# Attention beside a three-layer network: the network's matmuls in half-row pairs over two PSUM banks, and a new rule for when value products are taken

## The reference

```python
def _L0_attn_ref(x, w_qkv, b_qkv, w_out, b_out):
    qkv = x @ w_qkv + b_qkv
    q, k, v = jnp.split(qkv, 3, axis=-1)          # then 16 heads of 16 features
    scores = jnp.einsum('bhid,bhjd->bhij', q, k) * attn_scale
    scores = jnp.where(j >= i, scores, -jnp.inf)
    attn = jax.nn.softmax(scores, axis=-1)
    out = jnp.einsum('bhij,bhjd->bhid', attn, v)
    return out @ w_out + b_out

def _L0_ffn_ref(x, k0, k1, k2, s0, s1, s2):      # k0 512x1024, k1 1024x1024, k2 1024x256, all +-1
    h = jnp.concatenate([x, -x], axis=-1)
    h = s0 * _conn_dense(k0, h)
    h = jax.nn.relu(h) * 2
    h = s1 * _conn_dense(k1, h)
    h = jax.nn.relu(h) * 2
    return s2 * _conn_dense(k2, h)

xn = _layernorm(x, axis=-1)
x = x + _L0_attn_ref(xn, ...) * _silu(_L0_ffn_ref(xn, ...))
```

## Time and profile before

| what | us |
|---|---|
| time, median of 3 runs (lowest, highest) | 2429.61 (2428.54, 2431.49) |
| the profiled execution's own time | 2430.44 |
| its span, first to last instruction | 2428.7 |
| PE busy | 2363.3 |
| weight loads (PEld) busy | 1482.5 |
| DVE busy | 1792.3 |
| ACT busy | 1525.4 |
| POOL busy | 913.9 |

### The profile page before, as it was taken

How to read it: one execution, slowest core, us unless ns; L and a number is a source line. 1 busy time by engine, 2 the same in 40 slices (tenths; PEclk the granted TensorE clock), 3 DMA queues, 4 the chain that set the end, 5 groups by cost and what they waited for, 6 DMA issues and landing times.

```text
span 2428.7 us, 50993 instructions
## 1 busy us (share of the span) xinstructions
PE 2363.3 (97%) x17616; PEld 1482.5 (61%) x17616; DVE 1792.3 (74%) x4516; ACT 1525.4 (63%) x3135; POOL 913.9 (38%) x1080
## 2 busy tenths in 40 slices
PE   7999999999999999999999999999999999999995
PEld 6777666656565656565655656566665666555652
DVE  7767777777777777777877777777777777777732
ACT  5664656667666676666666666666666666666552
POOL 1005334343333434343434434353434444344533
PEclk9999999999999999999999999999999999999997
DMA  8983112020111212131212112221212212122222
GB/s 307 353 326 112 37 33 58 24 64 23 45 39 43 77 53 78 39 87 39 82 46 74 55 39 76 56 79 41 77 44 68 63 37 83 49 73 78 62 72 81
DMA packets 157805, 192.67 MB, mean 79 GB/s; under 512 B 65276, under 2 KB 102076, under 8 KB 157560
## 3 DMA queue, kind: packets, MB, share of 16 engines
q1 hardware_dynamic: 156600, 189.41, 25.4%
q10 hardware_dynamic: 960, 0.00, 0.0%
HBM read 112.13 MB, written 76.14 MB: 78 GB/s over the span
## 4 chain that ended last, share of the span: by engine, by line
PE 90%; DMA 4%; DVE 2%; issue 1%; SPq 1%; ACT 1%; POOL 1%; POOLq 0%; ACTq 0%; DVEq 0%
PE b_ps L1342 22%; PE b_pv_ps L1320 22%; PE b_ps L1300 15%; PE b_ps L1288 15%; PE b_ps L1346 5%; PE b_ps L1339 5%; DMA a_xs<-L_attn_x 3%; PE b_ps L1365 3%; PE a_qk_ps L290 1%; DVE a_stats L396 1%; DVE a_qk_parts L434 1%; PE b_ps L1308 1%; PE a_v_ps L300 0%; ACT b_probs L1400 0%; SPq L1133 0%
## 5 line engine op out<-in xcount | busy, mean ns | idle before, releaser
L1400 ACT ACTIVATE b_probs<-b_ps 128x512 f32<-128x512 f32 (+3 forms) x2560 | 1184.1, 541 | 622.2 <-PE b_ps L1288 613.3
L1455 DVE TENSOR_REDUCE b_part_max<-b_ps 128x1 f32<-128x512 f32 x1536 | 960.8, 680 | 279.2 <-PE b_ps L1300 276.0
L1452 DVE CUSTOM_DVE_ANT_0 b_ps<-b_ps,k_mask 128x512 f32<-128x512 f32 (+3 forms) x1024 | 477.2, 518 | 214.3 <-PE b_ps L1300 212.7
L1320 PE MATMUL b_pv_ps<-b_probs,k_vst 128*32 128x512 f32 (+3 forms) x5120 | 583.7, 540 | 0.6 <-ACT b_probs L1400 0.5
L1342 PE MATMUL b_ps<-b_u_hi,k_w 128*128 128x256 f32 x2048 | 535.6, 298 | 0.0
L1288 PE MATMUL b_ps<-k_qst,k_kst 50*128 50x512 f32 (+3 forms) x2560 | 503.5, 411 | 7.2 <-ACT b_u L1428 3.7
L1300 PE MATMUL b_ps<-k_kst,k_qst 48*128 48x512 f32 (+3 forms) x2560 | 494.5, 410 | 3.3 <-DVE b_part_max L1455 0.9
L1342 PE MATMUL b_ps<-b_u_lo,k_w 128*128 128x256 f32 x2048 | 497.3, 279 | 0.0
L1342 PEld LDWEIGHTS b_ps<-b_u_hi,k_w 128*128 128x128 f32 x2048 | 386.7, 189 | 81.1 <-issue 72.2
L1300 PEld LDWEIGHTS b_ps<-k_kst,k_qst 48*128 48x128 f32 x2560 | 234.6, 185 | 299.4 <-issue 152.1
L1288 PEld LDWEIGHTS b_ps<-k_qst,k_kst 50*128 50x128 f32 x2560 | 244.9, 185 | 255.4 <-ACT b_probs L1400 84.7
(11 more groups left out here) (105 smaller groups left out, 1847.8 us busy)
## 6 DMA issues: line engine op xcount, KB each, us to landing
qk_parts<-a_qk_parts SPq DMA_DIRECT2D x64, 512.0 KB, 3.9
k_kst<-qk_parts SPq DMA_DIRECT2D x384, 64.0 KB, 2.3
k_qst<-qk_parts SPq DMA_DIRECT2D x384, 64.0 KB, 2.3
a_xs<-L_attn_x SPq DMA_DIRECT2D x16, 512.0 KB, 6.0
xn_T<-a_xT SPq DMA_DIRECT2D x16, 512.0 KB, 5.8
v_plain<-a_v_out SPq DMA_DIRECT2D x16, 512.0 KB, 5.6
k_xf<-xn_T SPq DMA_DIRECT2D x32, 256.0 KB, 3.2
b_v_in<-v_plain SPq DMA_DIRECT2D x64, 128.0 KB, 2.7
```

The costliest lines, as they stand in the source:

```text
L1320: mm = pe.matmul(pv_ps[h * VW:(h + 1) * VW, 0:cols], vst[:, kb // TT, kb % TT, h, :], probs[:, s % P_SLOTS, h, 0:cols], start=start, stop= ...
L1400: act.activation(probs[:, s % P_SLOTS, h, 0:cols], ps[:, banks[place, half][0], 0:cols], ACT.Exp, scale=HD ** -0.5).then_inc(exp_done, 1)
L1452: dve.tensor_tensor_reduce(src, src, mask[:, 0:CHUNK - k0 % CHUNK], 1.0, -3.0e38, ALU.add, ALU.max, dst).then_inc(ring_read, 1)
L1455: dve.tensor_reduce(dst, src, AX_X, ALU.max).then_inc(ring_read, 1)
```

## The change

The network's blocks are cut in two halves of rows. A block's rows 0 to 63 and its rows 64 to 127 are two matmuls of 64 rows, as S and M have them, and since two row halves must not add into one bank at the same time, a use now has two banks: in the first half of the use, rows 0 to 63 add into the first bank and rows 64 to 127 into the second, for different output blocks; at half way they swap. So that the swap is safe, PE waits at half way for the last matmul of the first half (`f_half`). A use now covers four output blocks, 64 pairs in layer 1, 16 in layer 0 and 32 in layer 2, and there are five uses a piece, 160 in all. The matmuls of the network go from 6144 of 128 rows to 6144 pairs of 64 rows; the readers' work is the same but that the last layer's two ACT passes become four of half the width.

The plan's rules are new too. S, M and F are one mode now, and only V and the whole-array odds and ends change it. Values are taken once four steps wait, and then until none is left that is ready (`WAITING`, `LEFT`). Else the network goes first while it is behind its share, then an S or M pair if two banks are free, then the network, then values. A use of the network needs two free banks to begin.

```diff
-USES = KF // FPU
+F_BANKS = 2
+USES = KF // (F_BANKS * FPU)
...
+def network_pair(kind, j):
+    depth = KH if kind == "L0" else KF
+    phase, at = divmod(j, (1 if kind == "L2" else FPU) * depth * SPLIT)
+    return phase, at // (depth * SPLIT), at // SPLIT % depth, at % SPLIT
...
-        start = min(self.release)
+        start = sorted(self.release)[F_BANKS - 1]
...
-        if self.mode == "R":
-            self.begun = self.matmuls
-            if rows and pair <= now + self.STAY:
-                return "R"
...
+        if products and (waiting >= self.WAITING or self.mode == "V" and waiting > self.LEFT):
+            return "V"
+        if network and behind > 0:
+            return "F"
+        if rows and pair <= now:
+            return "R"
+        if network:
+            return "F"
+        if products and not (rows and pair <= now + 0.3):
             return "V"
...
-                    dst = f_bank(use)
+                    half_way = uses_of_network[use][3] // 2
                     for j in range(lo, hi):
...
+                        swapped, tile, f, part = network_pair(kind, j)
+                        if j == half_way:
+
+                            pe.wait_ge(f_half, use + 1)
+                        for n in range(F_BANKS):
+                            half = n ^ swapped
+                            rows = slice(half * HALF, (half + 1) * HALF)
...
+                                mm = pe.matmul(dst[:, tile], w[rows, f, m * P:(m + 1) * P], x_parts[part][rows, f, :],
+                                               start=first, stop=last, skip_group_check=True)
```

More of the change, by code:

```diff
@@ L627, in __init__ @@
         self.use = self.done = self.split = 0
-        self.matmuls = self.begun = 0
+        self.pairs = 0
         self.needed, self.split_at = {}, []
@@ L807, in take_network @@
                     self.emit(*event[2:])
-            self.take(("F", self.use), "f")
-        bank = self.banks["F", self.use][0]
-        count = min(count, total - self.done)
+            for n in range(F_BANKS):
+                self.take(("F", self.use, n), "f")
+        taken = [self.banks["F", self.use, n][0] for n in range(F_BANKS)]
+        count = min(self.QUANTUM, total - self.done)
         lo, self.done = self.done, self.done + count
@@ L821, in take_network @@
         if kind == "L2":
-            self.release[bank] = self.reads("ACT", self.clock["PE"], self.EXP, 1400)
-            self.clock["POOL"] = max(self.clock["POOL"], self.release[bank]) + 1.0
+            for bank in taken:
+                self.release[bank] = self.reads("ACT", self.clock["PE"], self.EXP, 900)
+            self.clock["POOL"] = max(self.clock["POOL"], self.release[taken[-1]]) + 1.0
             t = self.step()
@@ L829, in take_network @@
         else:
[L830 to L835, removed]
+            for bank in taken:
+                if self.split >= U_SLOTS:
+                    self.clock["ACT"] = max(self.clock["ACT"], self.split_at[self.split - U_SLOTS])
+                self.release[bank] = self.reads("ACT", self.clock["PE"], self.EXP, 640)
+                self.clock["POOL"] = max(self.clock["POOL"], self.release[bank]) + 1.95
+                self.split_at.append(self.clock["POOL"] + 0.1)
+                self.split += 1
             self.needed["L1" if kind == "L0" else "L2", k] = self.split
@@ L849, in choose @@
         waiting = self.scores // 2 - self.products
-        if self.mode == "R":
-            self.begun = self.matmuls
-            if rows and pair <= now + self.STAY:
-                return "R"
[L854 to L862, removed]
-            if products and waiting >= self.WAITING:
-                return "V"
-            if network:
-                return "F"
-        elif rows and free >= self.ENOUGH["V"]:
+        if products and (waiting >= self.WAITING or self.mode == "V" and waiting > self.LEFT):
[3 more added lines that the diff above has]
+        if rows and pair <= now:
             return "R"
-        if products:
+        if network:
+            return "F"
+        if products and not (rows and pair <= now + 0.3):
             return "V"
-        if network:
-            self.begun = self.matmuls
-            return "F"
-        return "R" if rows and pair <= now + 0.4 else None
+        return None
     def wait(self):
@@ L1325, in _ @@
                     if lo == 0:
-                        claimed(("F", use))
+                        for n in range(F_BANKS):
+                            claimed(("F", use, n))
                         if kind == "L0" and q == 0:
```

123 lines of the change are left out of this document (66 added, 57 removed).

## The result

The changed kernel takes **2475.85 us** (median of 4 runs, 2469.8 to 2480.05), the kernel before, run beside it, 2430.18 (4 runs, 2428.54 to 2431.49). The ratio is **1.0186**, 95% interval 1.0163 to 1.021: slower by 46 us, where 27 us less were forecast. It lies inside the range of the prediction, on the other side of no change.

A forecast was written before the change was run, and what follows sets the result against it. PE was taken as the bound, hardly ever idle in the second stage. The terms -224 + 6 + 20 + 180 + 31 - 40 = -27 took 2430.4 to 2403 us; forecast 2370 to 2435, whole range 2300 to 2525.

The forecast's parts named there:

- Changes of mode: PE's switches into R, the whole array and V become fewer, 374 us of cost down to 150: 224 saved.
- Half-row pairs: 6144 network matmuls become 6144 pairs of 256 columns, each 0.001 us dearer: +6 us, bounds 0 and 37.
- instruction issue: Rival: network pairs take four instructions for two, so 0.124 us a pair, 2434 us, about no change; chance 0.04.
- serial loads: Rival: the two halves' weight loads run one after the other, 657 us in place of 6, near 3050; chance 0.03.
- The wait at half way: PE waits 160 times, mid-use, for the first half's last matmul: +20 us, between 0 and 66.
- Pairs just in time: 1261 S and M pairs right behind a network pair, some with late weights: +31 us, between 0 and 126.
- late banks: The loader's 333 waits before S and M for a late bank in the kernel before go away: -40 us.
- The gaps: Between network uses PE runs short of banks while ACT and DVE read: +180 us, low bound 30, high bound 281.
- No time is to be had from the clock: PE's granted clock stood at 9 tenths or more in every slice but the last, so no gain there.
- The slower rival (2502): Gaps between uses and late pairs cost 238 us or more, against the forecast's 211: 2502 us; chance 0.37.
- The 0.09 behind a network pair: Sign: an S pair behind a network pair no longer pays the 0.09 us for leaving the network's mode.
- The loader's idle time before S and M: Sign: this idle time, released by ACT and DVE, rises from about 220 us by 150 or more, between uses.

The follow-up runs named there:

- the fastest kernel: The changed kernel with WAITING 5, LEFT 4 in place of 4, 0 (a single value step, only when five wait): 2370.35 us, ratio 0.976 to the kernel before.

## Why the prediction failed, point by point

**Changes of mode: -224 forecast, -223 to -226 found.** The prices from the earlier trace rows and the counts from the order were enough.

**Half-row pairs: +6 forecast, none found.** Pairs follow at 0.12 us (312.54 to 312.66), and 11 ns over the 107 of streaming fit the runs of pairs after as they fit the blocks before. Neither instruction issue nor serial loads showed.

**The wait at half way: +20 forecast, 14 to 17 found,** about 0.1 us a use; five or six uses touch low clock and are left out.

**Pairs just in time +31, late banks -40.** Together with the half-way wait and the pairs I had +17 within the uses; the excess there stayed the same (53.5 and 53.4; by the second sorting it fell by 9). The first term can be read from the trace: the 1031 S and M pairs that stand between network pairs of one use with no change of mode, the half-way places left out, hold 18 us of excess, where I had 31 for 1261. With the half-way wait that makes some 32 to 35, so 30 to 45 must have gone elsewhere within the uses, as the -40 has it. That is known by difference alone.

**The gaps: +180 forecast, +197 found,** about 207 with the waits that fall into low clock (204 and 217 by the second sorting). The account of the earlier trace rows against PE's own work was right to 10 or 20%, and the earlier trace rows, which spoke for 30, was rightly not followed: that stretch had begun with banks saved up.

**The clock: not in the sum, +66 found.** This is the step that failed: the sum has no term for the granted clock. "No time is to be had from the clock" is true of the earlier trace rows, and I read it as if none could be lost either. With the other terms as they came out the total would be -226 + 0 + 207 = -19, so 2411 against the 2403 of the forecast; with the clock it is +48. The trace of before had a warning. Windows before and after the clock falls in the middle of PE's one long wait for a reader:

```profile
core 0: us, PE busy (x) PEld busy (x) DVE busy (x) ACT busy (x) POOL busy (x), PEclk, DMA share, GB/s
2130.00:2141.20 11.20, 9.52 (x81) 6.30 (x79) 7.64 (x19) 6.20 (x12) 6.93 (x9) 1.00 0.07 15
2141.20:2148.00 6.80, 4.93 (x20) 3.78 (x20) 0.52 (x1) 3.23 (x7) 1.89 (x2) 0.50 0.31 87
```

And the timeline there:

```profile
2143.07 0.80 PE L1288 MATMUL b_ps<-k_qst,k_kst 50*128 50x512 f32 x2 [3.55 <-ACT b_u L1428]
2143.80 0.58 PE L1346 MATMUL b_ps<-k_w,b_u_hi 128*128 128x256 f32 x1
2144.18 0.41 PE L1346 MATMUL b_ps<-k_w,b_u_lo 128*128 128x256 f32 x1
2144.39 0.41 PE L1346 MATMUL b_ps<-k_w,b_u_hi 128*128 128x256 f32 x1
```

PE waited 3.55 us, up to 2143.07; the clock fell at 2141.2, within the wait, and PE then streamed at half speed, 0.21 us a matmul. I forecast 180 us of new waits and gave this no price. A third of the 66 us in the sum would have turned the forecast to no change (-27 + 22), and all of it to slower.

**The slower rival (2502).** The time went its way, but not by its mechanism: gaps and late pairs together came to some 215 to 235, under the 238 from which it was to decide, though not by much. What decided was the clock on top of them.

**The signs that I named.** Network pairs at 0.12: yes. The 0.09 behind a network pair is gone where the bank is free in time (312.06 to 312.23 still has 0.05 of it, as a late load). DVE's share of the second stage: 1663 of 2298 us, 72%, against 74% in the earlier trace rows; it fell, as it must where the time rises. The loader's idle time before S and M was a bad witness. Its causes before L1292 and then L1304, to be held against the earlier trace rows:

```profile
  ACT b_probs L1414: 81.0, 169
  DVE b_part_max L1472: 37.6, 89
...
  ACT b_probs L1414: 48.4, 117
  DVE b_part_max L1472: 19.5, 39
```

That is 187 us in 414 times where the earlier trace rows has 219 in 333: no rise (nor with the masked maxima, 230 against 243), although the gaps cost 200 more. The loader idles at every change of mode too, and of these more than half are gone (2066 before, 883 after); the one hid the other. Nor does PE's own idle time show all, 81 us against 11: a pair's record ends 0.17 us or more after the next could have started (0.40 long, 0.23 apart), so the first 0.17 of each wait looks like work. Only the distance from start to start has it whole.

**Still open:** which of the short waits bring the clock down. In the kernel that starts a use as soon as two banks are free the waits were longer in all, and it held. Nor can I say why the fastest kernel has 76 us of low clock where before has 54; 17 of these 22 us lie in its first 332 us, where before has 7 and it has 24.

## What to carry to other kernels

A change that trades changes of mode for waits has to be priced with the clock of the engine that waits: where the trace shows it at full speed, it shows what there is to lose. Ready work that needs no bank is what covers the readers' time, so keep some of it back and give it out in small pieces; keeping one to four steps was worth 84 to 105 us here, with the 30 to 82 us of added changes of mode already paid. And where a change has two parts, look at each with the other left out: here one was worth 1.9%, the other cost 3.5%, and the whole showed neither.

## What the chip showed that I had not expected

- The granted clock fell to 1.2 GHz with PE busy by its records for 4.5 of the 5.4 us before it, no idle time there over 0.52 us; by columns it had streamed for 2.7. In the whole trace the clock was low in 31 stretches, 197 us.
- Matmuls of zeros in the waits brought 123 of these back, and 24 us of time with 160 us of added work.
- Four instructions for a half-row pair stream as fast as two for a whole block, 0.12 us each over thousands.
- One bank of seven was worth 139 us (5.8%).
